# Moving every large SBUF tile that TensorE reads to a multiple of 1024 bytes

## What is computed

```python
x = x + L0_xattn(layernorm(x), fside, ctx)   # int8-like linear 256->256, silu(gate)*up, linear 128->256
x = x + L0_ffn(layernorm(x), w1, w2, w3)     # ternary weights; sigmoid(x1)*x2; 704 hidden
x = x + L1_xattn(layernorm(x), ctx, mask, Wq, Wk, Wv, Wo)   # 16 heads of 128, 8 key/value heads, softmax
x = x + L1_ffn(layernorm(x), router, shared and routed gate/up/down)  # 1024 shared + 128 routed hidden

# L1_xattn
scores = einsum('bhtd,bhsd->bhts', x @ Wq, ctx @ Wk) / sqrt(128)
out = einsum('bhts,bhsd->bhtd', softmax(scores), ctx @ Wv) @ Wo
# L1_ffn
h = silu(x @ gate.T) * (x @ up.T);  y = h @ down.T     # the routed part is scaled by the router's weights
```

## Time and profile before

| | us |
|---|---|
| median of 3 runs | 390.81 (390.16 to 391.75) |
| span of the profiled execution, first to last instruction | 388.6 |
| median less that span: what lies around the span | 2.2 |

### The profile page before, as it was taken

The page is one execution under the profiler, slowest core; times in us unless marked ns, Lnnn a source line. Parts: engine busy times, 40 slices in busy tenths (PEclk is TensorE's granted clock), DMA queues, the critical chain, the costliest instruction groups (busy, mean ns, idle before and its releaser), DMA issues.

```text
span 388.6 us, 8397 instructions
## 1 busy us (share of the span) xinstructions
PE 377.2 (97%) x2972; PEld 357.0 (92%) x2972; DVE 298.9 (77%) x978; ACT 233.3 (60%) x616; POOL 162.4 (42%) x260
## 2 busy tenths in 40 slices
PE   7898999999999999999999999999999999999996
PEld 6787898999899999999999999999999999999896
DVE  4687989889967889888767989887767876666644
ACT  1797787776644466766554466766554676664332
POOL 2113676875633343344543345245343333332232
PEclk9999999999999999999999999999999999999999
DMA  7999200000000200000000200000000000000000
GB/s 264 320 338 392 99 32 0 3 2 0 3 2 0 66 20 3 2 1 3 1 29 2 59 1 2 0 3 3 1 29 2 0 3 0 3 0 2 21 10 27
DMA packets 15193, 16.93 MB, mean 44 GB/s; under 512 B 1584, under 2 KB 14128, under 8 KB 15152
## 3 DMA queue, kind: packets, MB, share of 16 engines
q1 hardware_dynamic: 15152, 16.40, 13.2%
HBM read 15.34 MB, written 1.05 MB: 42 GB/s over the span
## 4 chain that ended last, share of the span: by engine, by line
PE 80%; DVE 8%; ACT 4%; DMA 3%; issue 2%; SPq 2%; POOL 1%; DVEq 0%; POOLq 0%
PE bank_qa L409 12%; PE bank_o L662 7%; PE bank_s L607 7%; PE bank_pt L627 7%; PE bank_u L643 7%; PE bank_s L409 5%; PE bank_o L666 4%; PE bank_s L615 3%; PE bank_u L647 3%; PE bank_s L526 3%; DMA wq_raw<-in_wqT 3%; PE bank_pt L409 3%; PE bank_u L747 3%; PE bank_pt L526 2%; PE bank_x L418 1%
## 5 line engine op out<-in xcount | busy, mean ns | idle before, releaser
L1312 POOL TENSOR_SCALAR prob<-prob,row_inv,valid_b 128x256 f32<-128x256 f32 x128 | 70.3, 559 | 84.9 <-DVE row_inv L1682 84.9
L1008 ACT ACTIVATE prob<-prob,row_min 128x256 f32<-128x256 f32 x128 | 64.2, 503 | 39.7 <-DVE row_min L1674 39.6
L1687 DVE TENSOR_TENSOR pt_lo<-bank_pt,pt_hi 128x512 fp32r<-128x512 f32 x64 | 43.9, 686 | 14.9 <-ACT pt_hi L961 14.9
L1674 DVE CUSTOM_DVE_ANT_0 prob<-bank_s,masked 128x256 f32<-128x256 f32 x128 | 48.5, 418 | 0.9 <-ACT masked L990 0.6
L1323 POOL TENSOR_TENSOR act_lo<-act_raw,act_hi 128x256 fp32r<-128x256 f32 x32 | 24.2, 755 | 44.4 <-ACT act_hi L1075 44.2
L961 ACT ACTIVATE pt_hi<-bank_pt 128x512 fp32r<-128x512 f32 x64 | 37.6, 587 | 4.1 <-PE bank_pt L627 3.8
L627 PE MATMUL bank_pt<-ident,prob 128*128 128x128 f32 x256 | 39.2, 274 | 0.4 <-POOL prob L1312 0.3
L607 PE MATMUL bank_s<-cxT_hi,qa_hi 128*128 128x256 f32 x128 | 37.9, 319 | 0.0
L409 PE MATMUL bank_qa<-xt_hi,a_hi 128*128 128x256 f32 x126 | 35.6, 283 | 0.0
L409 PE MATMUL bank_qa<-xt_lo,a_hi 128*128 128x256 f32 x126 | 35.5, 282 | 0.0
L409 PE MATMUL bank_qa<-xt_hi,a_lo 128*128 128x256 f32 x126 | 35.5, 281 | 0.0
(11 more groups left out here) (323 smaller groups left out, 1195.8 us busy)
## 6 DMA issues: line engine op xcount, KB each, us to landing
wq_raw<-in_wqT SPq DMA_DIRECT2D x4, 512.0 KB, 7.9
wo_raw<-in_wo SPq DMA_DIRECT2D x4, 512.0 KB, 8.8
w_raw<-in_w12T SPq DMA_DIRECT2D x2, 704.0 KB, 7.7
gate_raw<-in_gateT SPq DMA_DIRECT2D x2, 576.0 KB, 8.5
up_raw<-in_upT SPq DMA_DIRECT2D x2, 576.0 KB, 10.3
down_raw<-in_downT SPq DMA_DIRECT2D x2, 576.0 KB, 12.3
x<-in_x SPq DMA_DIRECT2D x4, 256.0 KB, 5.7
guT<-in_guT SPq DMA_DIRECT2D x4, 256.0 KB, 4.4
```

The costliest lines, as they stand in the source:

```text
L1008: act.activation(row, row, ACT.Exp, scale=-1.0, bias=row_min[:, h % 2, t:t + 1], accum_out=row_sum[:, h % 2, t:t + 1]).then_inc(S["s_exp"], 1)
L1312: pool.tensor_scalar(row, row, row_inv[:, h % 2, t:t + 1], valid_b[:, 0:1], ALU.mult, ALU.mult).then_inc(S["s_norm"], 1)
L1674: dve.tensor_tensor_reduce(out=prob[:, h % 2, t, :], in0=src[:, t * T:(t + 1) * T], in1=masked[:, :], scale=1.0, scalar=3.0e38, op0=ALU.ad ...
L1687: dve.tensor_tensor(pt_lo[:, :, cols], bank["pt"][:, :].rearrange("p (s t) -> p s t", s=2), f32(pt_hi[:, :, cols]), ALU.subtract).then_inc ...
```

## The change

Only the order in which tiles are made changes. Twelve small tiles come first (they fill bytes 16512 to 17407), the other small ones last. Every instruction on every engine is the same, in the same order, with the same semaphores and shapes; only addresses differ. Each DMA is the same as well, to another SBUF address.

```diff
+        router_raw = sb("router_raw", [P, ND, NR])
+        router = sb("router", [P, ND, 2 * NR], F32R)
+        scores8 = sb("scores8", [P, NT, NR])
+        half_exp = sb("half_exp", [P, 2, NB, ND])
+        mask8 = sb("mask8", [P, T], U8)
+        valid_b = sb("valid_b", [P, 1])
+        ln_stats = sb("ln_stats", [P, NT, 6])
+        ln_mv = sb("ln_mv", [P, NT, 2])
+        ln_ve = sb("ln_ve", [P, NT])
+        ln_rstd = sb("ln_rstd", [P, NT])
+        amax0 = sb("amax0", [P, 2, NB, ND])
+        ratio0 = sb("ratio0", [P, 2, NB, ND])
+
         with ExitStack() as raw:
             wq_raw = sb("wq_raw", [P, H, D], F32, raw)
...
         down_hi = sb("down_hi", [P, FFN_CHUNKS, D], F32R)
-        router_raw = sb("router_raw", [P, ND, NR])
-        router = sb("router", [P, ND, 2 * NR], F32R)
-        scores8 = sb("scores8", [P, NT, NR])
         w12 = sb("w12", [P, ND, 2 * BIT], F32R)
...
         ut_lo = sb("ut_lo", [P, 2 * T], F32R)
+
+        root0 = sb("root0", [P, 2, NB, ND])
+        lnq_stats = sb("lnq_stats", [P, NB, NT, 6])
...
+        top_w = sb("top_w", [P, NT, 2])
+        comb = sb("comb", [P, NT])
```

More of the change, by code:

```diff
@@ L186, in build @@
         ones = sb("ones", [P, P])
-        half_exp = sb("half_exp", [P, 2, NB, ND])
         x = sb("x", [P, NB, NT, D])
-        mask8 = sb("mask8", [P, T], U8)
-        valid_b = sb("valid_b", [P, 1])
         masked = sb("masked", [P, T])
[L194 to L197, removed]
         xt_hi = sb("xt_hi", [P, ND, T], F32R)
@@ L207, in build @@
         qw = sb("qw", [P, 4, D])
[L209 to L222, removed]
         wscale = sb("wscale", [P, D])
@@ L231, in build @@
         cxT_lo = sb("cxT_lo", [P, T], F32R)
[L232 to L239, removed]
         guT = sb("guT", [P, ND, 2 * I])
         logits = qw[0:2 * NR, 0, :]
[L243 to L246, removed]
         with ExitStack() as first:
@@ L268, in build @@
         ut_lo = sb("ut_lo", [P, 2 * T], F32R)
+        root0 = sb("root0", [P, 2, NB, ND])
+        lnq_stats = sb("lnq_stats", [P, NB, NT, 6])
+        lnq_mv = sb("lnq_mv", [P, NB, NT, 2])
+        lnq_rstd = sb("lnq_rstd", [P, NB, NT])
+        amax1 = sb("amax1", [P, 2])
+        ratio1 = sb("ratio1", [P, 2])
+        sis = sb("sis", [P, 2])
+        warm = sb("warm", [P, 2])
+        rowmax = sb("rowmax", [P, 4])
+        qscale = sb("qscale", [P, 2, 4])
+        qrecip = sb("qrecip", [P, 4])
+        row_min = sb("row_min", [P, 2, NT])
+        row_sum = sb("row_sum", [P, 2, NT])
+        row_inv = sb("row_inv", [P, 2, NT])
+        gsum = sb("gsum", [P, 6])
+        gam = sb("gam", [P, 6])
+        inv = sb("inv", [P, 3])
+        magic = sb("magic", [P, 1])
+        top8 = sb("top8", [P, NT, NR])
+        top_d = sb("top_d", [P, NT, 2])
+        top_w = sb("top_w", [P, NT, 2])
+        comb = sb("comb", [P, NT])
         S = {}
```

## The result

The changed kernel takes 392.62 us (median of 6 runs, 392.46 to 393.35), the kernel before 390.68 us in the runs beside it. The ratio is 1.0056, 95% interval 1.0036 to 1.0076: slower by 0.6%, or 1.9 us, just outside of what can be told from no change. The forecast was 393.7 us, 1.1 us more.

A forecast was written before the change was run, and what follows sets the result against it. TensorE's matmul spacing was taken as the bound: quick fp32r kinds turning slow add 3.2 us, nine tenths of it 2.9 us; 388.6 us of span becomes 391.5, with 2.2 us around it 393.7 us. Range 385.0 to 395.5 us.

The forecast's parts named there:

- TensorE's spacing is the time: Beyond the start, time is the number of matmuls times their spacing; TensorE busy 377.2 of 388.6 us.
- The cost comes from both starts together, not from either: For fp32r matmuls of 256 columns, streamed start less weights' start sorts quick from slow kinds; neither own start does.
- The rival in which a start at a multiple of 1024 helps: Streams starting at 0 avoid crossing into a further memory block: 388.2 us mildly, 381.6 us strongly; chance 0.25.
- its opposite: Rival B of the experiments, not the prediction: a tile's own start decides, and a multiple of 1024 is bad.
- "Difference modulo 128.": Start difference 0 modulo 128 makes fp32r pairs slow, 64 quick; the change makes all 0, adding 3.2 us of spacing.
- The slow spacing, 119.3 ns: Spacing that `yt`, `c`, `down` and `w3` products would reach: 1.64, 1.00, 0.39 and 0.16 us, sum 3.2 us.
- "Nothing for the slow kinds": `xt` (560 matmuls) and `cxT` (384) products keep difference 0, so they add nothing.
- Nine tenths on the path: TensorE has hardly any idle time to absorb the loss, so 2.9 of 3.2 us reach the time.
- The chances: Forecast 0.50, the two rivals 0.25 each; slower 0.43, faster 0.20, within 0.5% 0.37; a seventh of the forecast within 0.5%.
- Mix, bf16 products, transposes: nothing: `pt` with `cx`, bf16 products and some 500 transposes add 0; 1 us of transposes kept as an upper end.
- DMA: nothing: Raw weights landing at 0 instead of 128 modulo 1024 add 0, with -0.3 us as an end.
- The rule weighed against this: Weight loads take no read bandwidth from the running matmul, so sum 0; reason for the no-address rival, 390.8 us, chance 0.25.

The follow-up runs named there:

- the twelve runs: Twelve follow-up kernels with the same instructions in the same order, only tile starts differing; ratios to the kernel before from 0.9925 to 1.0074.
- step 0: Streamed start less weights' start is 0 modulo 256: the changed kernel, 1.0056 to the kernel before; with all large tiles 64 bytes further, 1.0066.
- step 192: Every streamed tile 192 bytes behind its weights modulo 512, against the kernel before: 386.49 us, ratio 0.9925; with large tiles 64 bytes further 387.94 us, 0.9931.
- step 64: Every streamed tile 64 bytes behind its weights modulo 512, against the kernel before: 389.64 us, ratio 0.9993.
- The first run: Changed kernel's order with gaps, weights at 0 and streams at 64 modulo 128, mixed modulo 256; against the kernel before: 388.99 us, ratio 0.9955.
- step 256: Every streamed tile 256 bytes behind its weights modulo 512, against the kernel before: 392.58 us, ratio 1.0074.
- steps 128, 160 and 224: Three kernels, every streamed tile that many bytes behind its weights, against the kernel before: ratios 1.0041, 1.0016 and 1.0028.

## Why the prediction was right, and where it was not

*TensorE's spacing is the time.* Right. The other engines' busy times moved by 0.3 us at most, and over the twelve runs the time follows the mean spacing, though not one for one: 114.8 ns gives 0.9925, 117.4 ns 0.9993, 119.6 ns 1.0056 to 1.0074.

*The cost comes from both starts together, not from either.* Right, and shown twice: all tiles moved by 64 bytes leave 119.6 ns at step 0 and 114.9 for 114.8 ns at step 192. The rival in which a start at a multiple of 1024 helps was wrong, and so was its opposite.

*"Difference modulo 128."* This was the wrong size of the rule. With one step everywhere the period is 256, and the steps 64 and 192, which I had put into one class, give 117.4 and 114.8 ns; 128, which I had put with 0, gives 118.7. That the rule was good enough was luck: every step became 0 in the changed kernel, and there both periods say the same.

*A pair's own step does not settle its spacing where steps are mixed.* In the kernel before `yt` had step 64; `c`, `down` and `w3` had 192; scores had 128; `xt` had 0. By the table `c`, `down` and `w3` should have been the quickest. Their means over the whole trace were 116.9, 116.8 and 117.4 ns, and `yt` had 116.1; with step 192 everywhere the same three run at 114.4 to 114.8 ns. The first run says so too. Its queries, all at step 192, take 116.7 ns (114.3 with step 192 everywhere), and its ternary-up products, all at step 64, take 116.4 ns (117.8 with step 64 everywhere). So the table is one of whole kernels with one step, and what the pairs around a pair do to it is open.

*The slow spacing, 119.3 ns.* A little low. Most pieces outside of waits are at 120.0 ns: 1.44 us for 12, 0.96 for 8, 0.48 + 0.24 for 6. By the means over the whole trace `yt` went from 116.1 to 119.7 ns, `c` from 116.9 to 119.8, `down` from 116.8 to 119.7, `w3` from 117.4 to 119.8; times their numbers that is 1.6 + 1.1 + 0.6 + 0.2 = 3.5 us where I had 3.2. (The few pieces that I had read for `yt` gave 115.5 ns, a little too quick.) "Nothing for the slow kinds" was nearly right: queries went from 119.1 to 119.6 ns, ternary-up from 119.2 to 119.8, together 0.3 us, and scores from 118.7 to 118.9. With these all the fp32r products of 256 columns grew by 3.9 us.

*Nine tenths on the path.* This is the term that failed. Of 3.9 us only 1.9 us arrived in the medians, 2.2 us in the profiled spans. By the trace, start to next start summed over each kind: `c` +0.94 us, `yt` with `gate` and `up` +1.34, `down` +0.32, `w3` 0.0, where spacing alone would give `down` and `w3` 0.6 and 0.2 us. The difference lies in spacings that hold a wait: a `down` or `w3` product waits for its `act` tile from ScalarE, VectorE or GpSimd, and when the products ahead of it take longer, it waits less. The transposes of `hs` took 0.42 us less; I put that down to the same, without a run that shows it. I read the idle column of the windows as if waits had to show there; a matmul that starts late behind another whose passage through the array still counts as busy shows as no idle time.

The start blurs the medians and spans. The chain's bf16 product at 76.47 us came at 76.18 us in the changed kernel, 0.3 us early, and in the kernel of step 256, with the same spacing, at 76.79 us; so I take it as no effect of the change. Free of the start is the stretch from TensorE's 201st matmul (30.34 us before, 29.98 after) to its last: 354.9 us before, 357.5 us in the changed kernel, 357.6 us at step 256. That is 2.6 us of the 3.9, two thirds. Over both kernels and the twelve runs this stretch grows by 0.59 us for every us by which the 2,113 spacings grow, and none lies more than 0.3 us from that line. So the pass-through was six to seven tenths, not nine. The two misses worked against each other: the spacings grew by more than my sum and less of it arrived.

*The chances.* One step of the reckoning was wrong: of an even spread from 1.9 to 3.6 us only a seventeenth lies below 2.0 us, and not a seventh. The measured 1.9 us lies just there.

*Mix, bf16 products, transposes: nothing.* Held: four mix products of 512 columns 0.93 us for 0.92, bf16 0.44 for 0.44 us. *DMA: nothing.* TensorE's 0.3 us wait for `wq_raw` is not among the changed kernel's waits, of which the shortest listed is 0.2 us; with one profile of each kernel, and a start that varies by more, nothing follows from it.

*The rule weighed against this.* The Trainium skill, page TensorE: Matmul & The Clock Gate, section Step-by-step, has weight loads take no read bandwidth from the running matmul. The runs do not contradict two ports, but the same instructions run at 114.8 or 119.6 ns a matmul with nothing changed except starts, so the rule's sum of 0 did not hold. It fits two reads that hinder each other by a few ns, but it does not show that. Every gap also moved the streams against the other engines' tiles, no run has TensorE alone, and where two accesses would meet the profile does not tell. I have shown the step, not the mechanism.

## What to carry to other kernels

Where TensorE runs pairs of a weight load and a matmul back to back, compare the spacing of equal matmuls between kinds before taking it as fixed; here 5 ns a matmul, 6 us or 1.5% of the kernel between steps 192 and 256 in the same set of runs, hang on where the tiles start. Aligning every tile to the same round number makes every step 0, which was the worst choice of those tried. Every streamed tile 192 bytes behind its weights modulo 256 was the best, 0.75% quicker than before; some pairs at 192 among others at 0, 64 and 128 did not get that spacing. And read how much of a busy engine's extra time will arrive from the waits that follow it, not from its idle time.

## What was not expected of the hardware

With one step for all pairs, the spacing of fp32r matmuls with 256 columns depends on that step with a period of 256 bytes and a narrow dip: 118.1 ns at 160, 114.8 at 192, 118.3 at 224. Products of 512 columns gain nothing at the dip: their spacing, the two or so with a wait left out, was 231.4 ns before and 232.5 ns at step 192. And at steps 0, 64 and 192 single matmuls have mainly three spacings, 113 to 114, 117 to 119 and 120 ns. A sequence mostly keeps one of them through a whole chunk and can change it at the next, with the same step; at step 0 only 1% are at 115 ns or below. At steps 128, 160 and 224 spacings from 115 to 122 ns stand within one chunk. What picks the one or the other is open; it was not tried apart from the starts.
